# Graph-transformer layer and graph-attention layer on one core: where the setup's loads, weight scalings and constants stand

## The reference, cut to what matters

```python
# layer 0
normed = layernorm(x, g1, b1)
q, k, v = normed @ Wq + bq, normed @ Wk + bk, normed @ Wv + bv      # 8 heads of 32
w = softmax(q @ k.T / sqrt(32) + 2 * adj - 1) * (0.25 + 0.75 * adj)
w = w / max(w.sum(-1), 1e-6)
x = x + (w @ v) @ Wo + bo
x = x + gelu(layernorm(x, g2, b2) @ Wf1 + bf1) @ Wf2 + bf2
# layer 1, two graph attentions
def graph_attention(y, W, a_src, a_dst):
    h = y @ W                                    # 8 heads, then 1 head
    e = leaky_relu((h @ a_src)[:, None] + (h @ a_dst)[None, :], 0.2) + adj
    return softmax(e) @ h
x1 = graph_attention(layernorm(x, lg1, lb1), W1, a_src1, a_dst1) + x
out = graph_attention(layernorm(x1, lg2, lb2), W2, a_src2, a_dst2) + x1
```

## Time and profile before

| | us |
|---|---|
| median of 3 runs | 1142.55 (1141.83 to 1142.95) |
| the profiled execution | 1142.3 |
| its span, first to last instruction | 1140.4 |
| busy: PE, PEld | 1080.7 (95%), 944.6 (83%) |
| busy: DVE, ACT, POOL | 776.0 (68%), 715.9 (63%), 405.7 (36%) |
| mean granted TensorE clock, share of full speed | 0.982 |

### The profile page before, as it was taken

The page is one execution under the profiler, slowest core; times in us unless marked ns, Lnnn a source line. Parts: engine busy times, 40 slices in busy tenths (PEclk is TensorE's granted clock), DMA queues, the critical chain, the costliest instruction groups (busy, mean ns, idle before and its releaser), DMA issues.

```text
span 1140.4 us, 41350 instructions
## 1 busy us (share of the span) xinstructions
PE 1080.7 (95%) x16172; PEld 944.6 (83%) x16172; DVE 776.0 (68%) x1908; ACT 715.9 (63%) x1702; POOL 405.7 (36%) x628
## 2 busy tenths in 40 slices
PE   5799999999999989999999999999999999889897
PEld 4688888888888878889988998998888888767775
DVE  5677777776777774554455545555788898858786
ACT  1467777677777664554355435546688888657663
POOL 1541121121211203232113211322478788775552
PEclk9799999999999999999999999999999999889899
DMA  8021011111010000000000000000000000001112
GB/s 223 18 76 30 30 30 56 32 30 30 30 39 11 13 2 1 1 1 1 0 0 0 0 0 0 0 1 10 21 21 18 28 18 20 5 20 61 68 55 93
DMA packets 41736, 31.18 MB, mean 27 GB/s; under 512 B 5280, under 2 KB 41376, under 8 KB 41632
## 3 DMA queue, kind: packets, MB, share of 16 engines
q1 hardware_dynamic: 36736, 28.84, 8.1%
q10 hardware_dynamic: 4896, 0.80, 0.6%
HBM read 21.25 MB, written 8.39 MB: 26 GB/s over the span
## 4 chain that ended last, share of the span: by engine, by line
PE 82%; DVE 7%; issue 5%; POOL 3%; ACT 2%; ACTq 1%; DVEq 0%; DMA 0%; POOLq 0%
PE BK L1333 6%; PE BK L1211 5%; PE BK L1210 5%; PE BK L1418 5%; PE BK L1417 5%; PE BK L1419 5%; PE BK L1209 5%; PE BK L1307 4%; PE BK L1319 4%; PE F L1209 3%; PE BK L1300 3%; PE F L1211 3%; PE F L1210 3%; PE F L1225 3%; PE BK L1479 3%
## 5 line engine op out<-in xcount | busy, mean ns | idle before, releaser
L1068 ACT ACTIVATE gf<-BK,bcol 128x512 f32<-128x512 f32 x128 | 88.1, 688 | 177.8 <-PE BK L1211 167.4
L862 POOL TENSOR_TENSOR ve<-mv,eps_l 128x4 f32<-128x4 f32 x64 | 14.0, 218 | 443.8 <-DVE mv L293 405.0
L987 ACT ACTIVATE e_sb<-BK,nmx 128x128 f32<-128x128 f32 x512 | 141.8, 402 | 28.5 <-DVE nmx L449 28.5
L1417 PE MATMUL BK<-wf_hi,gh 128*128 128x256 f32 x512 | 143.0, 279 | 0.0
L1418 PE MATMUL BK<-wf_hi,gl 128*128 128x256 f32 x512 | 141.5, 276 | 0.0
L1419 PE MATMUL BK<-wf_lo,gh 128*128 128x256 f32 x512 | 141.4, 276 | 0.0
L542 DVE TENSOR_TENSOR gl<-gf,gh 128x512 fp32r<-128x512 f32 x128 | 93.8, 732 | 63.2 <-ACT gh L1069 60.9
L455 DVE TENSOR_TENSOR pt_sb<-BK,ft 128x512 f32<-128x512 f32 x128 | 85.3, 687 | 67.6 <-PE BK L1307 66.1
L1007 ACT ACTIVATE xn<-x_all,neg_mr,rstd 128x256 f32 (+1 forms) x188 | 102.9, 602 | 19.7 <-POOL neg_mr L871 16.2
L573 DVE TENSOR_TENSOR x_all<-BK,x_all 128x256 f32 (+1 forms) x64 | 27.2, 425 | 113.9 <-PE BK L1419 113.9
L1211 PE MATMUL BK<-xh,wf_lo 128*128 128x512 f32 x256 | 100.8, 394 | 0.0
(11 more groups left out here) (206 smaller groups left out, 2888.2 us busy)
## 6 DMA issues: line engine op xcount, KB each, us to landing
x_all<-in_x_dram SPq DMA_DIRECT2D x16, 512.0 KB, 4.3
adj_in<-in_adj_dram SPq DMA_DIRECT2D x32, 256.0 KB, 2.8
out_dram<-y SPq DMA_DIRECT2D x16, 512.0 KB, 2.9
s_wf<-in_L_gnn_Wf_dram SPq DMA_DIRECT2D x2, 1024.0 KB, 11.8
s_w<-in_L_gnn_W_dram SPq DMA_DIRECT2D x2, 256.0 KB, 8.5
s_wq<-in_L_gnn_Wq_dram SPq DMA_DIRECT2D x1, 256.0 KB, 3.6
s_wk<-in_L_gnn_Wk_dram SPq DMA_DIRECT2D x1, 256.0 KB, 4.2
s_wv<-in_L_gnn_Wv_dram SPq DMA_DIRECT2D x1, 256.0 KB, 4.7
```

The lines of the kernel that those rows point to most:

```text
L987: e = act.activation(e_sb[:, j, :], LE[:, r, q, :], ACT.Exp, bias=nmx[:, j:j + 1], scale=1.0)
L1068: act.activation(gf[f % 2][:], BK[:, f % 4, :], ACT.Gelu, bias=bcol[:, 6 + f:7 + f])
L1417: pe.matmul(dst, gh[:, f, n], hi[:, f, :], start=(f == 0), stop=False)
```

## The change

It moves the setup's work, and leaves out none of it.

- Loads on SP: x and adjacency of tile 0 are first, then Wq, Wk, Wv, Wo, then x and adjacency of tile 1, and then, behind a wait for the first five columns, Wf1 and Wf2. W1, W2 and the four attention vectors are loaded after the end of stage A (the vectors on SP too, no longer on ScalarE). ScalarE issues first the five columns that the projections need, then two rows, then seven columns.
- Step 0 of A: TensorE turns tile 0 first and then multiplies the projection biases. VectorE takes the low part of x between the splits of Wq and Wk. `setup_rows` is gone from step 0.
- Step 1 of A: TensorE has the feed-forward biases (`setup_biases`: bv Wo and the products with Wf1) after its turn; VectorE adds them after two statistics; ScalarE makes the high part of Wf1 in the first half and of Wf2 in the second; GpSimd's gain of Wf1 is in step 0, behind the rstd of tile 1, and its two low parts at the end of step 1. TensorE waits for `setup_at["biases"]` before the second half.
- Stage B: VectorE's constants are seven pieces between residual sums in steps 0, 1 and 14; GpSimd has the gains of W1 and W2 in step 0 and their low parts in step 1; ScalarE has their high parts in step 0; TensorE has `setup_constants` in step 14, behind its third group, into the banks F[0] and F[1]; VectorE writes the last constants in step 15, and TensorE and ScalarE wait for them there.
- SP's wait for the setup stands in every odd step of A but step 1.

```diff
@@ VectorE
-            dve.wait_ge(w_in[3], 16 * len(small_cols))
-            dve.wait_ge(w_in[0], 64)
+            dve.wait_ge(w_cols, 16 * len(first_cols))
+            dve.wait_ge(w_qkv, 48)
             split("wq", 8)
+            ln_lo(CA)
             split("wk", 8)
             split("wv", 8)
...
+            def setup_biases():
+
+                dve.wait_ge(w_late, 16 * (len(later_cols) + 2))
+                dve.wait_ge(setup_pe, 2)
+                done(dve.tensor_tensor(bo_bc[:], BK[:, 5, 0:D], bo_bc[:], ALU.add))
+                done(dve.tensor_tensor(bcol[:, 6:14], BK[:, 4, 6:14], cols[:, 14:22], ALU.add))
+                setup_at["biases"] = steps[0]
...
                         a_ft_out(i, par)
-                        if first:
-                            setup_rows()
...
                         a_stats(i, half, par, (0, 1))
+                        if isinstance(i, int) and i == 1:
+                            setup_biases()
...
+                    if isinstance(i, int) and i == 0 and g < 3:
+                        (setup_marks, lambda: setup_sums(0, 0), lambda: setup_sums(0, 1))[g]()
+                    if isinstance(i, int) and i == 1 and g < 3:
+                        (lambda: setup_scores(0), lambda: setup_sums(1, 0), lambda: setup_sums(1, 1))[g]()
+                    if isinstance(i, int) and i == NC - 2 and g == 0:
+                        setup_scores(1)
@@ SP
-            for w, name in ((wq, "wq"), (wk, "wk"), (wv, "wv"), (wo, "wo")):
-                sp.dma_start(stage[name][:], kp(w)).then_inc(w_in[0], 16)
...
+                    for w, name in ((wq, "wq"), (wk, "wk"), (wv, "wv")):
+                        sp.dma_start(stage[name][:], kp(w)).then_inc(w_qkv, 16)
+                    sp.dma_start(stage["wo"][:], kp(wo)).then_inc(w_out, 16)
+                if isinstance(i, int) and i == 1:
+                    sp.wait_ge(w_cols, 16 * len(first_cols))
                     for w, name in ((wf1, "wf1"), (wf2, "wf2")):
-                        sp.dma_start(stage[name][:], kp(w)).then_inc(w_in[1], 16)
+                        sp.dma_start(stage[name][:], kp(w)).then_inc(w_ff, 16)
...
+            gate(a_x, NG)
+            for w, name in ((w1, "w1"), (w2, "w2")):
+                sp.dma_start(stage[name][:], kp(w)).then_inc(w_l1, 16)
+            for n, a in enumerate((as1, ad1, as2, ad2)):
+                sp.dma_start(a_bc[n][:], a.rearrange("h k -> (h k)").partition_broadcast(P)).then_inc(w_l1, 16)
@@ GpSimd
                     if first == CA and isinstance(i, int) and i == 0:
-                        setup_lo()
-                        pool.wait_ge(setup_dve, setup_at["all"])
+                        pool.wait_ge(w_ff, 32)
+                        setup_gain("wf1", 10)
+                        pool.wait_ge(setup_dve, setup_at["biases"])
                         add_bias(0, CA, bo_bc, a_xb)
+                    if first == CA and isinstance(i, int) and i == 1:
+                        setup_lo("wf1", False, 1)
+                        setup_lo("wf2", True, 2)
+                    if first == CB and isinstance(i, int) and i == 0:
+                        pool.wait_ge(w_l1, 16 * 6)
+                        setup_gain("w1", 24)
+                        setup_gain("w2", 28)
+                    if first == CB and isinstance(i, int) and i == 1:
+                        setup_lo("w1", False, 3)
+                        setup_lo("w2", False, 4)
@@ ScalarE
+                    if isinstance(i, int) and i == 1:
+                        if pp == 0:
+                            setup_hi("wf1", False, 1)
+                        else:
+                            setup_hi("wf2", True, 1)
...
+                if isinstance(i, int) and i == 0:
+                    setup_hi("w1", False, 5)
+                    setup_hi("w2", False, 5)
@@ TensorE
-                    if isinstance(i, int) and i == 1 and pp == 0:
-                        pe.wait_ge(setup_dve, setup_at["all"])
+                    if isinstance(i, int) and i == 1 and pp == 1:
+                        pe.wait_ge(setup_dve, setup_at["biases"])
...
                         ln_turn(i + CA)
+                        if first:
+                            setup_projections()
+                        if isinstance(i, int) and i == 1:
+                            setup_biases()
...
                             if first:
-                                pe.wait_ge(setup_dve, setup_at["projections"])
+                                pe.wait_ge(setup_dve, setup_at["splits"])
...
+                    if isinstance(i, int) and i == NC - 2 and g == 2:
+                        setup_constants()
```

More of the change, by code:

```diff
@@ L164, in build @@
         gf = [o(f"gf{r}", [P, W4]) for r in range(2)]
+        for name in ("w1", "w2"):
+            stage[name] = o(f"s_{name}", [P, KT, D])
+            scaled[name] = o(f"{name}_g", [P, KT, D])
+        a_bc = [o(f"a_bc{n}", [P, D]) for n in range(4)]
+        lb_wide = [o(f"lb_wide{n}", [P, KT, P]) for n in range(2)]
+        prod = o("prod", [P, KT, D])
+        wa = o("wa", [P, 2, 2, KT, H])
+        wag = o("wag", [P, 2, 2, KT, H])
+        wst = o("wst", [P, KT, P])
+        wc = o("wc", [P, 2, KT, P])
+        marks = o("marks", [P, 8])
         gt_all = overlay(at_wf1, at_wf1 + 4 * KT * FF * 4)("gt_all", [P, NG * P])
@@ L383, in setup_rows, with setup_sums @@
                 done(dve.scalar_tensor_tensor(out=row_cap[:], in0=marks[:, 7:8], scalar=RATIO_LIMIT, in1=row_cap[:], op0=ALU.mult, op1=ALU.add))
+            def setup_sums(layer, side):
+                name, heads = (("w1", H), ("w2", 1))[layer]
+                dve.wait_ge(w_l1, 16 * 6)
                 settle()
[L385 to L388, removed]
+                done(dve.tensor_tensor(prod[:], stage[name][:], a_bc[2 * layer + side][:].unsqueeze(1).to_broadcast([P, KT, D]), ALU.mult))
+                settle()
+                done(dve.tensor_reduce(wa[:, layer, side, :, 0:heads], prod[:].rearrange("p k (h d) -> p k h d", h=heads), AX, ALU.add))
@@ L493, in a_step @@
                         a_max(sp, 0)
-                    if pp == 0:
+                    if pp == 0 and not first:
                         ln_lo(i + CA)
@@ L783, in a_step @@
                     load_a(i + 1, half + par, 1 - par)
-                if isinstance(i, int) and i == 1:
-                    sp.wait_ge(setup_dve, setup_at["all"])
-                    sp.wait_ge(setup_act, setup_act_steps)
-                    sp.wait_ge(setup_pool, setup_pool_steps)
+                if par == 1 and not (isinstance(i, int) and i == 1):
+                    sp.wait_ge(setup_dve, setup_at["biases"])
+                    sp.wait_ge(setup_act, 2)
+                    sp.wait_ge(setup_pool, 3)
                     sp.wait_ge(setup_pe, 2)
@@ L929, in _ @@
                 if first == CC:
+                    pool.wait_ge(setup_dve, setup_at["all"])
                     pool.wait_ge(ln_xn, (CC + 1) * G)
@@ new lines, in broadcast_row @@
+            def broadcast_row(dst, wide_b, name):
+                for kt in range(KT):
+                    r = pe.matmul(dst, wide_b[:, kt, :], stage[name][:, kt, :],
+                                  start=(kt == 0), stop=(kt == KT - 1), skip_group_check=True)
+                return r
+            def setup_biases():
+                pe.wait_ge(setup_dve, setup_at["wide"])
+                pe.wait_ge(w_out, 16)
+                pe.wait_ge(w_ff, 32)
+                pe.wait_ge(w_late, 16 * (len(later_cols) + 2))
+                broadcast_row(BK[:, 5, 0:D], bv_wide, "wo")
+                for m in range(FT):
+                    r = bias_column(BK[:, 4, 6 + m:7 + m], stage["wf1"], m * P, 12)
+                r.then_inc(setup_pe, 1)
@@ L1408, in b_step @@
                     wide(BK[:, f % 4, :], "wf1", f * P).then_inc(b_h, 1)
+                if isinstance(i, int) and i == NC - 1:
+                    pe.wait_ge(setup_dve, setup_at["all"])
                 ln_turn(i + CB + 1)
```

228 lines of the change are left out of this document (101 added, 127 removed).

## The result

Over six runs of each kernel the median went from 1142.54 to 1134.12 us (1131.29 to 1137.44). The ratio is 0.9921, with a 95% interval of 0.9904 to 0.9937. The forecast was 1132.0, in a range of 1127 to 1137. The profiled execution took 1134.18 us with a span of 1132.3, 8.1 less than before.

The account below looks back on a forecast made before the run. TensorE's order was taken as the bound (82% of the chain of waits), broken in the setup. Gain 17.1 us less 1.3 (ScalarE), 1.7 (clock), 2.7 (moved matmuls), 1.3 (GpSimd) is 10.1: 1132.0 us, range 1127 to 1137.

Parts of the forecast that it names:

- The opening: Start of step 0: x loaded first and turned before the projection biases; adjacency turn at 17.9 against 19.78, gain 1.9 us.
- the table load "near 10.8": ScalarE in the opening: with 14 loads in place of 18, its table load starts near 10.8, not 12.87.
- Step 0 to step 1: TensorE's setup biases cover the copies and idle gaps close; adjacency turn of step 1 at 36.1 against 51.02, 14.9 us.
- The first half of step 1: Attention stage: 6.8 us in place of 9.0 without idle time and clock loss; a clock fall charged separately at 1.7 us.
- the light stretch ahead of it: Reason for charging 1.7 us: a lightly busy TensorE stretch before was followed by a clock fall, and the new one is light.
- ScalarE's high parts: Step 1, attention: high part of Wf1 covered, that of Wf2 before V's copies costs 1.2 to 1.3 us (bounds 0 and 1.9).
- The moved matmuls: Feed-forward stage: eight one-column and eight broadcast instructions on TensorE cost 2.7 us, with nothing to hide them.
- GpSimd beside VectorE's normalising: Feed-forward steps 0 and 1: GpSimd's gains and low parts delay VectorE's normalising; 1.3 us taken, bounds 0 and 3.2.
- the strict bound of 3.2: Feed-forward steps 0 and 1: VectorE always waits for GpSimd under an exclusive port lock; costs 3.2 us, time 1134.
- Rival (2): Strict-bound contention, half clock lasting twice as long, opening gaining only 1.0: gain 5.6 us, time 1136.7; chance 0.15.
- Rivals (3): Step 1 waited for statistics through a late x load; only idle gaps close, it ends within 2 us of before; chance 0.03.
- (4): Slower: one-column matmuls amid full work drop the clock lastingly; a feed-forward step costs 22.8 us, about 1155; chance 0.03.

Follow-up runs that it names:

- e3: The changed kernel with the seven later columns issued by SP behind Wf1 and Wf2, no longer by ScalarE; median 1130.89 us.
- e9: The changed kernel with Wf1 and Wf2 loaded ahead of x and adjacency of tile 1, as before the change; single run 1135.54 us.
- e5: The kernel before, with tile 1's statistics ahead of VectorE's constants and its rstd ahead of GpSimd's weight gains; span of a single run 1155.1 us.
- e1: The changed kernel with GpSimd's gains and low parts of W1 and W2 moved behind its bias sum of tile 1 in the feed-forward stage; median 1131.53 us.
- e8: The changed kernel run and profiled again, unedited, on the same chip as another run; median 1133.90 us.

## Why the prediction was right, point by point

The number is right, and so are the main mechanism and the forecast costs by kind. Their sizes are in part off, in both directions, and partly cancel.

**The opening: 1.9 us forecast, 0.9 measured.** The step that failed is the table load "near 10.8". x was there at 5.3 and normalised at 9.96, better than the forecast 10.5, and the adjacency turn came at 16.82, not 17.9. For the table load I took four loads of 0.46 us off 12.87, which is 11.0 and not 10.8, and let the other 14 loads issue as fast as before. They took 12.6 us in place of 10.1, the last four 5.5 (3.54 and 2.00). So the table load stood at 13.37, and the splits behind the low part of x became last. The text had a late queue as a bound ("a ScalarE queue that stays late to 12.8 gives 1.0 us"); e3, which takes the columns off that queue, moved the first projection to 17.70. The forecast 18.65 was passed in one execution with the queue as it is, e9, whose table load stood at 11.96.

**Step 0 to step 1: the turn at 36.1 forecast, 36.30 measured.** The time lost in the opening was mostly won back here, 0.8 us: ScalarE's last copy was over as the logits ended, so the gap of 0.4 before the turn of tile 1 did not come, and that turn and the bias group took 5.3 us (31.01 to 36.30) in place of 5.65. That TensorE stood for VectorE's constants, and that a swap of order is no cure with the loads as they were, is shown by e5. The new wait for the biases and the load of Wf1 cost nothing, as forecast.

**The first half of step 1: 6.8 us and 1.7 for the clock forecast, 8.6 measured.** The sum was right, its parts less so. A fall costs 1.3 us there by e1, not 1.7, and most of the 0.5 us of idle time that the forecast took out stayed (8.26 us busy of 8.60). The reason given, the light stretch ahead of it, is not shown: e1 has the same order and kept its clock.

**ScalarE's high parts: 1.3 us forecast.** The first cost nothing. The second made TensorE wait 0.56 us before the turn at 57.68. The head start at the adjacency turn of step 2 was 14.6 us, where the forecast has 17.1 - 1.3 - 1.7 = 14.1.

**The moved matmuls: 2.7 us forecast, 2.9 measured.** The residual sum at 765.77 waits 5.02 us in place of 2.29, 2.7 more, and the whole stretch is 2.9 longer. Nothing hides them. VectorE's seven pieces between residual sums made TensorE wait for none of the sums, as forecast.

**GpSimd beside VectorE's normalising: 1.3 us forecast, 2.2 measured, in steps that lengthened by more.** The four TENSOR_SCALARs took 1.49 and 1.87 us longer. TensorE's turns followed the start of normalising by 2.93 and 3.31 us, against 2.01 before, so they were 0.9 and 1.3 us late. That is the term, mis-sized by 0.9. I took the middle between nothing and the strict bound of 3.2, with the reason that VectorE's running operations let GpSimd in only in part. In the traces it is GpSimd that holds VectorE: of the two operations of 427.03 each kept one TENSOR_SCALAR until its end, and the other two ran free. The whole lengthening was 3.4 us in the first profile, 2.3 in e8, and at most 3.7 (e3) where GpSimd's work stood in the same place. e1, which only moves GpSimd's work, gave 1.7 to 2.8 back. The trace agrees with the rule of the Trainium skill, in "SBUF — State Buffer", section "SBUF: two separate sides", that the first to start keeps the port pair for its whole instruction. That the strict bound gave 1134, which is what was measured, is luck: it charges 3.2 where the turns were 2.2 late, and the rest came from matmuls further apart and from the last two stages. e5 shows the hold at its largest, with products of 0.69 us that took 3.53 and 4.16.

**The sum.** Forecast 10.1, measured 8.1 in the span and 8.4 between the medians. Against the forecast 2.1 us went in the first three feed-forward steps (0.9 of them the mis-sized wait), 0.2 in the moved matmuls and 0.4 in the last two stages; 0.8 came back at ScalarE's second high part. The opening's 1.0 was mostly won back by step 1. The forecast of a feed-forward stage longer by 3 to 4 us was too low, it was 6.3. Rival (2) described the late opening and a dearer contention, but not the long half clock, and lies on the other side of the result. Rivals (3) and (4) did not come: the turn of step 1 was 14.7 us ahead, and the clock was full from the second insertion to the end of the stage. The forecast said nothing of how far the last two stages vary by themselves, by up to 4 us in the profiles here, half of the gain; that the two profiles compared differ by only 0.4 there is luck.

## What to carry to other kernels

Setup work that stands in the order of the bounding engine is moved behind its first data, and the work that feeds it off the engine that must deliver that data; here 14.6 us came of it, and 2.9 were paid again as bare matmul time where the same products went. Where GpSimd gets such work, it is placed where TensorE is not waiting for what VectorE does beside it: the same gains and low parts made TensorE's turns 2.2 us late beside the normalising, and made it wait for nothing from 431.83 on, behind it (e1). When loads are reordered, the queue of the engine that issues them is read too: behind ScalarE's last small load stood the whole opening (e3). Where an effect is smaller than the spread of single runs, the unedited kernel is profiled a second time: here that set 1.1 us of a supposed cost apart (e8).

## What the runs showed of the hardware that was not expected

- Seven small column loads behind five others and two rows kept ScalarE from its first instruction until 13.37 us, in other executions until 11.96 to 14.34; without them it was free at 4.51.
- A reorder of the kernel before that should have helped cost 14.7 us. VectorE waited 6.14 us for x, and then its 128x512 products took 3.53 and 4.16 us beside GpSimd operations of 3.60 and 4.76 us that had started first.
- With one order of instructions at that place the granted clock fell in five executions and not in a sixth.
- At the full granted clock the same 154 matmuls of a feed-forward step took 22.76 us in some steps and 23.30 in others, with no idle time between them; why is open. In the last two stages the same 6764 matmuls had 323.3 us of busy time at a mean grant of 0.96 and 327.1 at 0.94.
